# Image recurrence: two matmuls of constants on TensorE ahead of each block's turning of gathered rows, into the PSUM bank that the turning overwrites

## The reference

```python
h = _L0_tok_ref(x, ...)                       # shifted window attention, gives the tokens
h = jnp.concatenate([cls, h], axis=1)
h = h + _L0_attn_ref(_layernorm(h), ...)      # gated linear recurrence
h = h + _L0_ffn_ref(_layernorm(h), ...)       # switch: each token goes to one of 8 experts
h = h + _L1_attn_ref(_layernorm(h), ...)      # recurrence over the 16 images
h = h + _L1_ffn_ref(_layernorm(h), ...)       # slice attention

def _L1_attn_ref(x_in, W_ih, W_hh, b_ih, b_hh):
    xp = jnp.einsum('tbi,hi->tbh', x_in, W_ih) + b_ih + b_hh
    def step(h, xp_t):
        h_new = jnp.tanh(xp_t + h @ W_hh.T)
        return (h_new, h_new)
    _, hiddens = jax.lax.scan(step, h0, xp)   # 16 steps, one for each image
    return hiddens
```

## Time and profile before

| | |
|---|---|
| median of 3 runs | 4369.61 us (4355.78 to 4375.41) |
| the profiled execution's own time | 4352.22 us, span 4350.4 us |
| TensorE busy | 3192.8 us, 73% of the span |
| GpSimd, VectorE, ScalarE busy | 59%, 58%, 49% |
| mean granted TensorE clock | 0.859 |

### The profile page before, as it was taken

The page is one execution under the profiler, slowest core; times in us unless marked ns, Lnnn a source line. Parts: engine busy times, 40 slices in busy tenths (PEclk is TensorE's granted clock), DMA queues, the critical chain, the costliest instruction groups (busy, mean ns, idle before and its releaser), DMA issues. The chain is left out here.

```text
span 4350.4 us, 68616 instructions
## 1 busy us (share of the span) xinstructions
PE 3192.8 (73%) x25552; PEld 1809.5 (42%) x25552; DVE 2524.8 (58%) x3049; ACT 2137.7 (49%) x3049; POOL 2570.2 (59%) x1541
## 2 busy tenths in 40 slices
PE   8999996999999940000099946666666899999998
PEld 6777774455555520000034312222221455555556
DVE  7888886988888851000055513333337777777772
ACT  6666675777777720000034435556552444444444
POOL 7777773877788716777600065555506666666661
PEclk9999998999999965555599957877777999999999
DMA  1111111122222121111133323333330122112211
GB/s 42 38 40 40 40 40 57 58 73 86 70 77 75 46 69 38 40 45 35 21 108 109 100 61 100 96 94 99 93 94 21 41 55 55 52 50 56 54 48 41
DMA packets 301346, 267.20 MB, mean 61 GB/s; under 512 B 99368, under 2 KB 229580, under 8 KB 300957
## 3 DMA queue, kind: packets, MB, share of 16 engines
q1 hardware_dynamic: 264718, 228.51, 17.3%
q0 software_dynamic: 25600, 21.10, 2.7%
q10 hardware_dynamic: 10704, 13.20, 0.9%
HBM read 127.66 MB, written 140.20 MB: 62 GB/s over the span
## 5 line engine op out<-in xcount | busy, mean ns | idle before, releaser
L1512 POOL DMA_INDIRECT D_row<-yb,D_idx x400 | 381.9, 955 | 628.3 <-DMA D_prob<-keepp 349.6
L2150 POOL TENSOR_TENSOR E_w<-E_w,E_rs 128x1024 f32<-128x1024 f32 x200 | 380.2, 1901 | 366.8 <-DVE E_rs L2073 366.8
L1241 POOL DMA_INDIRECT xb<-R_row,R_si x400 | 388.9, 972 | 212.4 <-issue 121.5
L1314 PE MATMUL X_px<-X_ident,X_xs 128*128 128x128 f32 x256 | 42.9, 291 | 558.6 <-DMA X_xs<-xb 558.6
L180 POOL TENSOR_TENSOR A_kmask<-A_ksb,A_pack_a 128x3584 f32<-128x3584 f32 x56 | 356.4, 6364 | 152.5 <-ACT A_ksb L327 152.5
L1373 ACT ACTIVATE X_hm<-X_ph,X_b 128x512 f32<-128x512 f32 x128 | 88.0, 688 | 594.6 <-PE X_ph L1326 594.6
L2058 DVE TENSOR_REDUCE E_mx<-E_lg 128x16 f32<-128x1024 f32 x200 | 244.8, 1224 | 220.3 <-PE E_lg L1867 220.1
L1388 DVE COPY X_xt<-X_px 128x512 f32<-128x512 f32 x64 | 43.6, 681 | 530.1 <-PE X_px L1314 530.1
L2144 POOL TENSOR_TENSOR E_hs<-E_w 128x512 f32<-128x512 f32 x200 | 254.7, 1274 | 97.1 <-ACT E_w L2031 97.1
L1879 PE MATMUL E_z<-E_w,E_yk 128*64 128x512 f32 (+1 forms) x800 | 223.7, 632 | 78.1 <-POOL E_w L2150 77.8
L1314 PEld LDWEIGHTS X_px<-X_ident,X_xs 128*128 128x128 f32 x256 | 27.5, 143 | 607.3 <-DMA X_b<-in_e_b 558.8
(11 more groups left out here) (292 smaller groups left out, 8412.6 us busy)
## 6 DMA issues: line engine op xcount, KB each, us to landing
xb<-B_blank SPq DMA_DIRECT2D x64, 256.0 KB, 3.9
X_xs<-xb SPq DMA_DIRECT2D x64, 256.0 KB, 2.8
yb<-X_ys SPq DMA_DIRECT2D x64, 256.0 KB, 2.0
B_x<-h SPq DMA_DIRECT2D x25, 512.0 KB, 4.3
h<-B_hh SPq DMA_DIRECT2D x25, 512.0 KB, 3.7
y<-B_yt SPq DMA_DIRECT2D x25, 512.0 KB, 2.6
R_row<-y SPq DMA_DIRECT2D x25, 512.0 KB, 3.4
A_xg<-in_xw SPq DMA_DIRECT2D x56, 224.0 KB
```

Of the source, the lines that this page charges most:

```text
L1241: pool.indirect_dma_start(out=xb, out_offset=bass.IndirectOffsetOnAxis(ap=si[:, B * c + b:B * c + b + 1], axis=0), in_=row[c % U][:, D * r ...
L1512: pool.indirect_dma_start(out=row[n % LR][:, k, b], out_offset=None, in_=yb, in_offset=bass.IndirectOffsetOnAxis(ap=idx[:, c, i:i + 1], ax ...
L2150: TT(w3, w3, bc(rs[g % 3][:].unsqueeze(2), [128, 2 * SH, G]), ALU.mult).then_inc(w_done, 1)
```

## The change

A new step `keep_going(t)` runs on TensorE in each block's iteration between `turn_y(t-5)` and `turn_rows(t)`. It waits for what `turn_rows` waits for of the bank (`x_done`, and `yk_done` from the sixth block on), but not for `sc_done`, and multiplies the identity by the first 512 columns of the constants twice, each time into the whole bank `D_pt` with `start=True`. `turn_rows` then overwrites the bank. Nothing reads what the two matmuls write, and they raise no semaphore.

```diff
+                def keep_going(n):
+                    after(pe, x_done, n)
+                    after(pe, yk_done, min(n - 4, N))
+                    for _ in range(2):
+                        mm(pt[:], ident[:], pack[:, 0:W], start=True, stop=True)
+
                 def center_in(n):
                     pe.wait_ge(x_done, n + 1)
                     after(pe, y_done, n - 1)
...
                 for t in range(N + 5):
                     at(turn_y, t - 5)
+                    at(keep_going, t)
                     at(turn_rows, t)
                     at(center_in, t)
                     at(inputs, t - 1)
```

## The result

The changed kernel takes 4408.99 us (median of 5, 4397.7 to 4415.6) beside 4370.86 us for the kernel before (median of 5): a ratio of 1.0089, 95% interval 1.0067 to 1.0111. That is 38 us more. It lies in the stated range (4287 to 4445 us); the likeliest case had been +2 us and no change that can be told, and what came is on the side of the third rival, slower.

A forecast was written before the change was run, and what follows sets the result against it. No engine was full: a PE and DVE chain set short blocks, POOL's gather runs the long pairs. Blocks at -10 us and pairs at +12 us gave +2 on 4369.6, about 4372 us; range 4287 to 4445 us.

The forecast's parts named there:

- the likeliest case: Whole kernel: filler and clock cancel, POOL's runs set the rest; +2 us, about 4372 us, own range 4350 to 4392; chance 0.36.
- the third rival: Slower: filler stays on the path and phase worsens, +27 to +75 us, or a third long pair, 54 us; chance 0.34.
- The sum of +2 us: Recurrence stage: 24 blocks outside the pairs at -0.4 us (-10 us) and 16 pairs at +0.75 us (+12 us).
- the forecast case: Whole kernel: no change that can be told, within about 0.5%, 22 us; chance 0.36.
- The filler's place and price: Ahead of each turning: two matmuls behind the `D_yk` copy take 1.72 us, delaying a wide block's turning 1.12 us.
- The clock: Ordinary blocks: the matmuls fill PE's 1.38 us hole, so the clock should be 0.95 or more there.
- What the clock gives back: Ordinary blocks: full clock returns 1.8 us at most, 1.5 as a mean, for a net of -0.4 us a block.
- The pairs keep their length: Long pairs of blocks: POOL's run sets 27.3 or 25.5 us; bounded by 0 and 3 us more, 0.75 taken.
- Its deciding point for the main branch: Third rival: whether the clock still falls; then 24 blocks pay 27 us and 16 pairs up to 48 us.
- The second rival: Faster: wide blocks of 10.2 us make POOL pause and long pairs rarer; half gone, 62 us less, 4307 us; chance 0.30.
- POOL's run as the cause of the late results: Long blocks: PE's results are held up until the run of 16 gathers has landed, tanh starting 2.6 to 2.9 us later.

The follow-up runs named there:

- one_nogather: One 512-column matmul in place of the changed kernel's two, gathers for the first four blocks alone; late chip: 4164.0 us beside 4361.2 for the kernel before, ratio 0.9556.

## Why the prediction was right and where it was not

The direction was left open, and the range held, but its width did more for that than the sum: it covers 158 us and three cases at about a third each. The sum of +2 us was off by 36 us, beyond the 22 us that the forecast case allowed. By its steps:

- **The filler's place and price.** Right in kind. The matmuls start behind the copy and take 1.79 us (1.72 reckoned), and the turning is 1.28 us later (1.12).
- **The clock.** Right: 1.00 in 28 of the 36 ordinary steps of the changed trace, and in 52 of 55 on a prompt chip. By the rule against long idle gaps alone (the Trainium skill, "TensorE: Matmul & The Clock Gate", section "Why this matters for your kernels") there would have been no gain in clock; filling a hole of 1.4 us raised it in every version run.
- **What the clock gives back: mis-sized.** I took 1.5 us for every ordinary block. On prompt chips, where nothing else interferes, the stage grew by 19.3 us. The price there is 55 x 1.28 = 70 us, so some 51 us came back, 0.9 us a block (the short blocks' higher price and the hidden first ones left aside). A block below full clock does get back 1.6 to 1.7 us, but on these chips 24 of the 55 steps before were at full clock already and had nothing to get back; 31 x 1.65 = 51 us, as an estimate, accounts for what came back. The prediction had written that such blocks run at 0.83 as often as at 1.00 and took 1.5 us for all of them even so. (In the trace that it read, it was not as often: 6 of the 41 ordinary steps were at 1.00.) On prompt chips the net is +0.35 us a block (9.35 to 9.70) where -0.4 was forecast.
- **The pairs keep their length: this step failed.** I wrote "so it keeps its 27.3 or 25.5 us unless the chain is so far behind then that more of it is left" and took 0.75 us for 16 pairs, 12 us. In the traces the long steps went from 14 to 19 and from 18.3 to 19.3 us. Five more at 9 us above an ordinary step are 45 us, one more us for each of 14 is 14 us, the others gave back 0.16 x 41 = 7 us: +52 us, and the stage grew by 52.8. In POOL's terms, 16 gathers on end came 18 times and not 13. The filler puts the turning 1.3 us later into POOL's run and adds four pieces ahead of it; the turning itself now came late, where before it was mostly the results behind it. That these two are the reason was not tested by a run of its own.
- **The third rival** named the other way to this side, a block drawn under 10.3 us and a third pair in place of 20.5 us. The block from 2904.7, at the place in the pair where the earlier trace rows has 11.4 us, takes 10.2 us, and the next one, 9.1 us before, 18.5 us. That is this rival as it stood, though a third long block comes in some pairs of images only, not in all eight. Its deciding point for the main branch, a clock that falls, was not met.
- **The second rival** had 10.2 us as a gain: POOL would pause in each block. It pauses for 0.46 us (2915.15), too little, as was said against it. The rival also took 10.2 us for every wide block. That is the length at two of the seven places; at the others it is 9.0 to 9.8 us, and the mean of 9.64 us on a prompt chip lies under the 10.0 us that eight gathers take.
- **POOL's run as the cause of the late results** was a pattern in the rows when I wrote. `one_nogather` shows the gathers as a cause on a late chip. What I missed is that the chip has a part in it as well: with 400 gathers on end a prompt chip has no late result. And "held up until the run of gathers has landed" is not what the semaphore records show. In the block from 2838.7 the semaphores of `inputs`, `center_out` and `first_hidden` rise at 2847.25, 2849.36 and 2851.46, one after another, the first of them before POOL's run ends; the turning of the changed kernel came at 2923.58 and POOL's last gather went out at 2923.91.

Why PE's results are late on some chips during gathers stays open. No run tells a held-up signal from slow work on PE, or says what differs between the chips. The growth with the number of pieces speaks for a price on each piece, and is no proof of it. That POOL's pausing helps was not tried there. One more trait of the late traces may bear on it: records are missing from them. Of the 497 semaphore updates that TensorE's instructions in this stage raise, the late trace of the kernel before holds 310 and that of the changed kernel 342, while the prompt ones hold 494 and 497; those of VectorE and ScalarE are thinned in the same way. Whether the recording itself has a part in the lateness was not tested either.

## What to carry to other kernels

Filler work on TensorE can hold its clock, but it should end before the instruction behind it could start: beside a weighing of 0.6 us, 0.51 us of matmul cost nothing in a wide block and 1.79 us cost 0.5% of the kernel on a chip with nothing else amiss. Before costing an edit to a chain, ask which engine's floor lies just under it: here the gathers' 9.15 us a block swallowed what a faster chain gave. And where blocks of one loop differ twofold in the trace, the edit's effect on how many are long weighs more than its effect on an ordinary one, and the same program should be measured on more than one chip.

## What the runs showed of the hardware that was not expected

- The kernel before took 4181 to 4184 us on two chips and 4361 to 4371 us in the other sets. All of the 4% lies in one stage (514 us for 683), in which indirect gathers run beside TensorE; the stages ahead of it (2518 and 2522 us) and behind it (1149 us in both) take the same time.
- On a late chip VectorE waited 8.7 and 13.6 us for a turning, in the blocks shown, while a row of gathers ran or just behind it; without gathers there was no long step from the seventh block on. Of 31 runs of 16 gathers in the traces of the two kernels, 30 had a step of 15 us or more.
- Transposes kept the granted clock at 1.00 as matmuls did (blocks of 9.0 and 9.5 us with either; 0.94 and 0.95 over the ordinary steps).
- The clock over the stage rose with the filler in small steps, 0.88, 0.93, 0.95 and 0.98, for 0, 0.51, 0.93 and 1.79 us of it a block.
